# Graph layer and mixture of experts on one core: second LayerNorm in two groups, early lists for six experts, table of the others filled later

## What is computed

```python
x = x + _L0_gnn_ref(_layernorm(x), edge_attr_512, path_coeffs, src, dst, path_indices)
x = x + _L0_ffn_ref(_layernorm(x)[None], Wr, sWg, sWu, sWd, Wg, Wu, Wd)[0]
...
    for e in range(NS):                       # NS = 2
        shared = shared + _swiglu_ffn(x, sWg[e], sWu[e], sWd[e])
    probs = jax.nn.softmax(x @ Wr, axis=-1)
    top_w, top_i = jax.lax.top_k(probs, K)    # K = 6
    top_w = top_w / jnp.sum(top_w, axis=-1, keepdims=True)
    gate = zeros.at[arange(N)[:, None], top_i].set(top_w)
    for e in range(E):                        # E = 64
        routed = routed + _swiglu_ffn(x, Wg[e], Wu[e], Wd[e]) * gate[:, e:e + 1]
    out = shared + routed + x
```

## Time and profile before

| | us |
|---|---|
| three runs | 1150.21, 1144.15, 1149.42 |
| their median | 1149.42 |
| the profiled execution | 1146.11 |
| its span | 1144.6 |
| TensorE busy | 910.4 (80%) |
| VectorE busy | 565.3 (49%) |
| ScalarE busy | 226.8 (20%) |
| GpSimd busy | 345.8 (30%) |
| mean granted TensorE clock | 0.946 of full speed |

### The profile page before, as it was taken

The page is one execution under the profiler, slowest core; times in us unless marked ns, Lnnn a source line. Parts: engine busy times, 40 slices in busy tenths (PEclk is TensorE's granted clock), DMA queues, the critical chain, the costliest instruction groups (busy, mean ns, idle before and its releaser), DMA issues.

```text
span 1144.6 us, 20271 instructions
## 1 busy us (share of the span) xinstructions
PE 910.4 (80%) x7172; PEld 495.2 (43%) x7173; DVE 565.3 (49%) x1321; ACT 226.8 (20%) x578; POOL 345.8 (30%) x390
## 2 busy tenths in 40 slices
PE   0267665775766757778899999999998999999982
PEld 0033333343433333447446454554644545454460
DVE  6277989879879798966611111112111121211126
ACT  1031321321313212123112111112111121211100
POOL 4705234243252342001232332333321332332110
PEclk9978898989889889999999999999998999999997
DMA  8826465465474654565699999999999999999747
GB/s 260 312 78 216 153 200 197 160 208 198 143 239 143 209 174 158 186 254 198 227 382 379 396 394 391 397 383 389 396 391 405 394 393 395 395 389 393 304 115 215
DMA packets 70389, 320.80 MB, mean 280 GB/s; under 512 B 12981, under 2 KB 13134, under 8 KB 48363
## 3 DMA queue, kind: packets, MB, share of 16 engines
q1 hardware_dynamic: 47351, 259.35, 60.4%
q0 software_dynamic: 21232, 56.55, 15.0%
q10 hardware_dynamic: 1668, 3.03, 0.9%
HBM read 308.30 MB, written 13.57 MB: 281 GB/s over the span
## 4 chain that ended last, share of the span: by engine, by line
PE 61%; DVE 12%; issue 9%; DVEq 5%; DMA 4%; another core or an unknown queue 4%; ACT 2%; POOL 1%; SPq 1%; POOLq 0%
PE ps L1219 19%; PE ps L1265 10%; DVE big L594 9%; PE ps L613 7%; PE ps L846 5%; PE ps L1163 3%; PE ps L664 3%; PE ps L873 3%; DVEq L585 2%; DVEq L592 2%; DMA big<-y_d 2%; PE ps L648 2%; PE ps L1212 2%; PE ps L632 1%
## 5 line engine op out<-in xcount | busy, mean ns | idle before, releaser
L594 DVE TENSOR_TENSOR big<-big 128x512 f32 (+1 forms) x640 | 384.8, 677 | 79.4 <-remote 43.4
L613 PE MATMUL ps<-big,mixed 128*32 128x256 f32 x2512 | 175.2, 407 | 96.9 <-DVE big L594 68.8
L1219 PE MATMUL ps<-big 128*64 128x512 f32 x1024 | 238.9, 609 | 13.5 <-issue 12.4
L333 POOL DMA_INDIRECT big<-xn_d,idx x157 | 166.4, 1060 | 266.5 <-DVE big L594 207.7
L1119 POOL DMA_INDIRECT big<-h_d,idx x64 | 62.5, 977 | 359.1 <-issue 274.6
L613 PEld LDWEIGHTS ps<-big,mixed 128*32 128x32 f32 x2512 | 81.7, 115 | 186.1 <-issue 82.3
L1229 DVE TENSOR_TENSOR mixed<-big,ps 128x256 f32<-128x256 f32 x64 | 27.0, 421 | 267.4 <-ACT big L1226 267.0
L1219 PEld LDWEIGHTS ps<-big 128*64 128x64 f32 x1024 | 69.0, 139 | 138.4 <-issue 132.7
L1265 PE MATMUL ps<-big,mixed 128*64 128x256 f32 x1024 | 126.3, 389 | 0.2 <-issue 0.2
L1180 POOL DMA_INDIRECT y_d<-big,sia x74 | 75.2, 1017 | 129.1 <-DVE big L1278 67.2
L623 ACT ACTIVATE mixed<-ps 128x512 f32<-128x512 f32 x40 | 23.9, 597 | 318.3 <-PE ps L613 282.6
(11 more groups left out here) (206 smaller groups left out, 669.7 us busy)
## 6 DMA issues: line engine op xcount, KB each, us to landing
big<-in_L_ffn_Wg SPq DMA_DIRECT2D x64, 1024.0 KB
big<-in_L_ffn_Wu SPq DMA_DIRECT2D x64, 1024.0 KB
big<-in_L_ffn_Wd SPq DMA_DIRECT2D x64, 1024.0 KB
big<-in_edge_attr SPq DMA_DIRECT2D x39, 1024.0 KB
big<-y_d SPq DMA_DIRECT2D x10, 672.0 KB
big<-xn_d,idx POOLq DMA_INDIRECT x157
big<-in_L_ffn_sWg SPq DMA_DIRECT2D x2, 1024.0 KB, 4.8
big<-in_L_ffn_sWu SPq DMA_DIRECT2D x2, 1024.0 KB, 6.9
```

The source lines that it names most:

```text
L333: pool.indirect_dma_start(xs[s][:, c, :], None, xn_d[:, :], bass.IndirectOffsetOnAxis(ap=table[:, c0 + c:c0 + c + 1], axis=0)).then_inc(x_ ...
L594: ins = dve.tensor_tensor(pr[k % 2][:, 0:chunks, EXT * p:EXT * (p + 1)], xs[s][:, 0:chunks, ds(o1, EXT)], es[s][:, 0:chunks, ds(o2, EXT)], ...
L613: ins = pe.matmul(bank(BA)[WIN * h:WIN * (h + 1), h0:h0 + HP * EXT], onehot[s][:, CW * h + r, :], pr[k % 2][:, CW * h + r, :], start=r == ...
L1219: ins = pe.matmul(bank(k2)[TA * h:TA * (h + 1), :].rearrange("p (w f) -> p w f", w=2), xgT[k2][:, k, 0:TA], gu[:, :, k, W * h:W * (h + 1)] ...
```

## The change

The second LayerNorm is taken apart into statistics(b), spread_of(g) and normalise(g) and run over two groups of blocks, 0 to 2 and 3 to 4. KA becomes 6: lists of six experts come from marks. KF = 4 keeps the first four picks where they were, and two more stand behind the shared expert's pieces. The two products of entries for codes and gates become one over a joint tile worth. entries(1) to entries(5) and enter(1) to enter(5) move later, one step of items apart. The gathers of items 4 and 5 wait for the marks' lists and no longer for the table; those of 6 to 9 stand behind take_table.

```diff
@@ -72,7 +72,8 @@
     UG = EXT // FPP
     CAP = -(-N // TB) * TB
     MAXB = CAP // TB
-    KA = 4
+    KA = 6
+    KF = 4
     YR = 8
...
@@ -794,7 +795,42 @@
             dve.wait_ge(added_ok, nput - (NG * NB - 1))
         VV(add_block(b))
 
-    ln2 = layer_norm(lambda b: H[:, b, :], add_messages)
+    def statistics(b):
+        add_messages(b)
+        V(dve.bn_stats(bn6[:, b, :], X[:, b, :]))
+
+    def spread_of(g):
+        V.own()
+        for b in range(g.start, g.stop):
+            V(dve.bn_aggr(mv[:, b, :], bn6[:, b, :]))
+        V.own()
+        VV(dve.tensor_scalar(st[:, 0, g], mv[:, g, 1], EPS, None, ALU.add))
+        after(act, V)
+        A(act.activation(st[:, 1, g], st[:, 0, g], ACT.Sqrt))
+        return A.n
+
+    def normalise(g, a_root):
+        ve, r0, r1, tmp = (st[:, k, g] for k in range(4))
+        dve.wait_ge(A.sem, a_root)
+        VV(dve.reciprocal(r1, r0))
+        VV(dve.tensor_tensor(tmp, r1, r1, ALU.mult))
+        VV(dve.tensor_tensor(tmp, tmp, ve, ALU.mult))
+        VV(dve.tensor_scalar(tmp, tmp, -0.5, 1.5, ALU.mult, ALU.add))
+        VV(dve.tensor_tensor(r1, r1, tmp, ALU.mult))
+        for b in range(g.start, g.stop):
+            ln2.append(V(dve.tensor_scalar(H[:, b, :], X[:, b, :], mv[:, b, 0:1], st[:, 2, b:b + 1],
+                                           ALU.subtract, ALU.mult)))
+
+    ln2 = []
+    g0, g1 = slice(0, 3), slice(3, NB)
+    for b in range(3):
+        statistics(b)
+    a_root0 = spread_of(g0)
+    statistics(3)
+    normalise(g0, a_root0)
+    statistics(4)
+    a_root1 = spread_of(g1)
+    normalise(g1, a_root1)
     V(dve.tensor_scalar(lin[:, 0, :], st[:, 2, :], 1.0, None, ALU.add))
     V(dve.scalar_tensor_tensor(lin[:, 1, :], mv[:, :, 0], -1.0, st[:, 2, :], ALU.mult, ALU.mult))
     v_lin = V.n
...
@@ -1002,13 +1038,16 @@
 
     def list_products(e0, e1):
 
-        o = bank(BH if e0 == 0 else 0)[0:TB, C * e0:C * e1].rearrange("p (e c) -> p e c", c=C)
+        o = bank(0 if e0 == 1 else BH)[0:TB, C * e0:C * e1].rearrange("p (e c) -> p e c", c=C)
+        if e0 == KF:
+            after(pe, A, a_list[0])
         for e in range(e0, e1):
             pick(e, o[:, e - e0, :])
-            shared_up_part(0, BEU, 1, 17 + 2 * e, 19 + 2 * e)
-            if e > 0 and e + 2 < KA:
+            if e < KF:
+                shared_up_part(0, BEU, 1, 17 + 2 * e, 19 + 2 * e)
+            if e > 0 and e + 2 < KF:
                 mark(e + 2)
-        if e1 == KA:
+        if e1 == KF:
             shared_up_part(0, BEU, 1, 25, len(UP))
         after(dve, T, t_list[e1 - 1])
         V(dve.tensor_scalar(idx_1[:, e0:e1], o[:, :, 0], float(OFF), None, ALU.add))
@@ -1027,7 +1066,11 @@
     v_flags = V.n
     list_products(0, 1)
     mark(2)
-    list_products(1, KA)
+    list_products(1, KF)
+    mark(KF)
+    mark(KF + 1)
+    list_products(KF, KA)
+    V(dve.tensor_copy(worth[:, :, 1, :], vals[:, :, 1:1 + TOPK]))
     table = bank(BEG)[0:TB, 0:2 * E]
     v_entry = {}
     en_ok = sem("en_ok")
@@ -1039,8 +1082,8 @@
         VV(dve.tensor_tensor(hot, idxf[:, :, k:k + 1].broadcast_to([BP, NB, E]),
                              ioe[0:BP, :].unsqueeze(1).broadcast_to([BP, NB, E]), ALU.is_equal))
         VV(dve.tensor_tensor(lgs[:, :, 0:E], hot, rk, ALU.mult))
-        V(dve.tensor_tensor(entry[k % 2][:, :, 0, :], hot, codes[:, :, k:k + 1].broadcast_to([BP, NB, E]), ALU.mult))
-        V(dve.tensor_tensor(entry[k % 2][:, :, 1, :], hot, vals[:, :, 1 + k:2 + k].broadcast_to([BP, NB, E]), ALU.mult))
+        V(dve.tensor_tensor(entry[k % 2], hot.unsqueeze(2).broadcast_to([BP, NB, 2, E]),
+                            worth[:, :, :, k:k + 1].broadcast_to([BP, NB, 2, E]), ALU.mult))
         VV(dve.tensor_reduce(desf3[:, :, k], lgs[:, :, 0:E], axis=AX.X, op=ALU.add))
         VV(dve.scalar_tensor_tensor(rank6[:, :, k], idxf[:, :, k], -float(CAP), desf3[:, :, k], ALU.mult, ALU.add))
...
@@ -1133,12 +1176,11 @@
             rows_of(TA)
 
     entries(0)
-    entries(1)
     v_two = early_pairs(0, KA)
     pool.wait_ge(s_h, n_h)
     after(pool, V, v_idx[0])
     gather(0, 0, 0)
-    after(pool, V, v_idx[KA - 1])
+    after(pool, V, v_idx[KF - 1])
     for s in range(1, 4):
         gather(s, s, s)
     for s in range(4):
@@ -1285,7 +1327,6 @@
         transpose_rows(4 * i + 1, 1, 16 * i + 16)
         if at(i, 0):
             enter(0)
-            enter(1)
         transpose_hidden(4 * i, 0)
 
     def quad(i, left, at_=None, up=None, dn=None):
@@ -1293,7 +1334,7 @@
         for s in range(4):
             t = 4 * i + s
             a = t if at_ is None else at_ + s
-            if s + 6 < left and not at(t, 0, 1, 2):
+            if s + 6 < left and not at(t, 0, 1, 2, 3):
                 pool.wait_ge(tr_ok, t + 3)
                 gather((s + 2) % 4, t + 6, t + 6)
             if s + 1 < left:
@@ -1304,17 +1345,22 @@
                 transpose_rows(t + 2, (s + 2) % 4, 16 * q + 16)
             if at(t, 0):
                 v_spread[0] = spread(v_two, 0, KA, first_two)
-            if at(t, 1):
-                enter(4)
+            if at(t, 3):
                 enter(5)
                 v_entry[TOPK] = take_table()
-            if at(t, 2):
+            if at(t, 4):
                 v_spread[1] = spread(v_entry[TOPK], KA, E, two)
             down(t, s, a, 32 * i + 32, 16 * i + 16)
             if at(t, 0):
+                enter(1)
+                entries(2)
+            if at(t, 1):
                 enter(2)
+                entries(3)
+                entries(4)
+            if at(t, 2):
                 enter(3)
-                entries(4)
+                enter(4)
                 entries(5)
             if at(t, 4):
                 after(pe, V, v_entry[TOPK])
@@ -1328,10 +1374,12 @@
                 shared_add(dn, BEG)
             if s + 1 < left:
                 transpose_hidden(t + 1, (s + 1) % 4)
-            if at(t, 1):
+            if at(t, 0):
+                after(pool, V, v_idx[KA - 1])
+            if at(t, 3):
                 after(pool, V, v_entry[TOPK])
-            if at(t, 1, 2):
-                for n in (4, 5, 6, 7) if at(t, 1) else (8,):
+            if at(t, 0, 3):
+                for n in (4, 5) if at(t, 0) else (6, 7, 8, 9):
                     pool.wait_ge(tr_ok, n - 3)
                     gather(n % 4, n, n)
             if at(t, 0, KA):
@@ -1339,8 +1387,7 @@
             scatter(t, s, a)
 
     first_items(0)
-    entries(2)
-    entries(3)
+    entries(1)
     VV(dve.tensor_scalar(cs_[4][:, 0:MAXB - 1], iotaw[:, 1:MAXB], float(TB), None, ALU.mult))
     VV(dve.tensor_tensor(cb, cnt[:, :].unsqueeze(2).broadcast_to([P, E, MAXB - 1]),
                          cs_[4][:, 0:MAXB - 1].unsqueeze(1).broadcast_to([P, E, MAXB - 1]), ALU.is_gt))
```

4 lines of the change are left out of this document (2 added, 2 removed).

## The result

| | before | changed |
|---|---|---|
| median of six runs | 1148.39 us | 1157.8 us |
| lowest to highest | 1144.15 to 1150.21 | 1152.2 to 1167.13 |
| ratio of the times | | 1.0075, interval 1.0047 to 1.0103 |
| the profiled execution, its span | 1146.11, 1144.6 | 1152.2, 1150.8 |
| mean granted TensorE clock | 0.946 | 0.935 |

The changed kernel is slower by more than the 0.5% that can be told apart, and 1157.8 us lies above the range that was predicted. The profiled execution is the fastest of its six, 6.1 us above the profiled one of before.

The account below looks back on a forecast made before the run. TensorE was taken to set the pace up to 870 us, so item 6's shift reaches the end: +0.5 at item 1, -4.5 to item 4, +4.05 to item 6, taken as +1.0 with slow work; 1149.4 + 1.0 = 1150.4 us, range 1144 to 1155.5.

Follow-up runs that it names:

- the six marks with the old table: Kernel before with six lists from marks and early gathers of items 4 and 5, its own table schedule and LayerNorm kept: 1083.59 us, ratio 0.9996.
- the weights held: Changed kernel, expert 7's down weights load held until item 6's gather landed: 1.0014, again 0.9991; also with one-group LayerNorm and item 0's rows before five shared pieces: 0.9990.
- seven marks: Changed kernel with item 6's list from marks too (KA = 7) and its gather issued at item 1: 1085.63 us, ratio 0.9988 to before.
- the cover and the moved product: Kernel before, item 0's rows transposed ahead of the last five shared pieces and Silu, VectorE's shared-unit product behind the entries: 1146.17 us, 0.9982; again 1081.49 us, 0.9975.
- one piece behind each pick: Changed kernel with seven marks, one LayerNorm group, one shared piece behind each pick, item 0's rows transposed ahead of the last eight pieces: 1149.84 us, 1.0011.

## What to carry to other kernels

The landing of a small gather beside large loads was a range here and not a value, 5.3 to 9.7 us with the table where it was before; if somebody waits for it, price both ends and the slow work behind the wait before a step is moved towards it. The small transfer that somebody waits for goes ahead of the large one that nobody waits for yet: one wait on the issuing queue gave back all that this change had lost. Where two engines hand work to each other, ask of each instruction in the queue of the one that sets the pace whether anybody needs it yet: in one trace each, moving one product behind the entries gained 4 us at item 6, where the six marks with the old table gained 3.5 for far more work. Neither gain is clear in the time.

## What the hardware showed that was not expected

The same gather of up to 96 rows, from POOL's issue to the use of its rows, took at most 3.0, 3.4 and 3.9 us in the three traces with the weights held, and 5.3 to 9.7 beside a load whose first part (Wd, 1 MB) SP had issued 0.35 or 0.7 us ahead. How busy the engines had been does not decide it alone. In the 2 us ahead of POOL's issue their share was 0.74 to 0.85 for the four gathers with the late table (6.8 to 9.4 us), and 0.04 to 0.08 for six that took 5.3 to 6.3, but 0.08 also for the one that took 9.7, and 0.79 or 0.80 for the three beside held weights. What goes with the landing is the length of SP's next issue, of Wg: 1.1 to 1.7 us in all seven traces with a landing of 5.3 to 6.8, and 0.47 to 0.50 in all four with 7.7 to 9.7. SP's issues for before and for the changed kernel (578.85 above):

```profile
562.41 0.38 SPq L718 DMA_DIRECT2D big<-in_L_ffn_Wd  x1
562.83 1.47 SPq L714 DMA_DIRECT2D big<-in_L_ffn_Wg  x1
```

Two more gathers, which nobody waited for, fit: 6.5 us beside an issue of 1.59 (seven marks) and 7.0 beside one of 0.47 (old table). It looks as if one of the two gets its packets in first, the gather or the next megabyte; that is a guess. The traces show the two going together, and none shows which is the cause.

TensorE's granted clock halves (1.2 instead of 2.4 GHz) for a spell of 3 to 10 us between the lists and item 1, most often from 30 or from 37 us behind the mark on, twice over in four traces. It does so in all traces but five: the kernel before with the cover and the moved product (twice), with the product alone, with the two-group LayerNorm, and the changed kernel in one of its three. What it costs hangs on what it meets: 1.5 to 1.9 us over the 18 pieces, 0.4 to 3.0 over item 0's gate and up, 2.6 over item 1's, 5 in the run with one piece behind each pick. The same kernel had it and had it not, so that a difference of 3 us at item 0 between two single traces says nothing about an edit. What decides it wasn't found.
